# Reordering VectorE and pacing the dummy matmuls in the first slots of a fused attention and ternary FFN kernel

## The reference

```python
def xattn(x, context):                       # IMG_LEN = 257 > 128 rows: all context rows are "image" rows
    q = rms_norm(linear(x, q_w, q_b), norm_q_w).reshape(B, L, 16, 32)
    k = rms_norm(linear(context, k_img_w, k_img_b), norm_k_img_w).reshape(B, -1, 16, 32)
    v = linear(context, v_img_w, v_img_b).reshape(B, -1, 16, 32)
    return linear(softmax(q @ k.T / sqrt(32)) @ v, o_w, o_b)      # the text part has no rows

def ternary(w):                              # groups of 64 weights
    scale = clip(mean(abs(w), group), 1e-08, None)
    return clip(round(w / scale), -1, 1) * scale

x = x + tanh(g_xattn) * xattn(layernorm(x), ctx)
h = square(relu(layernorm(x) @ ternary(W_fc).T))                  # 512 -> 2048
x = x + tanh(g_ffn) * (rms_norm(h) @ ternary(W_proj).T)           # 2048 -> 512
```

## Time and profile before

| | |
|---|---|
| median of 3 runs | 1003.59 us (1002.85 to 1004.45) |
| profiled execution, its own time | 1004.31 us |
| its span from first to last instruction | 1002.5 us |
| mean granted TensorE clock | 0.973 of full speed |
| PE busy | 928.4 us (93%) |
| PEld busy | 570.9 us (57%) |
| DVE busy | 689.4 us (69%) |
| ACT busy | 717.6 us (72%) |
| POOL busy | 565.7 us (56%) |
| chain that ended last | PE 82%, issue 6%, DVE 4%, ACT 4%, POOL 2%, DMA 1% |

### The profile page before, as it was taken

One profiled execution on the slowest core, in us unless ns is written; L12 is line 12 of the kernel. 1 busy time (PEld: TensorE's weight loads), 2 busy tenths in 40 slices (PEclk: granted clock), 3 DMA queues, 4 the chain that ended last, 5 costly groups with the idle time before them and its releaser, 6 DMA issues.

```text
span 1002.5 us, 26078 instructions
## 1 busy us (share of the span) xinstructions
PE 928.4 (93%) x9941; PEld 570.9 (57%) x10043; DVE 689.4 (69%) x1360; ACT 717.6 (72%) x1235; POOL 565.7 (56%) x616
## 2 busy tenths in 40 slices
PE   3676687899999999999999999999999999999998
PEld 1343344566656566666656656666665666666664
DVE  7988987876767676777677676767777676766400
ACT  2877766677777777777777777778777777776673
POOL 1223323755666566765657565766656665766484
PEclk9887887999999999999999999999999999999999
DMA  8635333333233444343323344433342344322100
GB/s 303 168 97 147 96 86 63 64 73 77 68 72 75 86 85 75 77 80 74 80 64 73 77 85 85 75 77 84 67 79 69 72 78 86 65 54 54 43 22 32
DMA packets 184588, 82.43 MB, mean 82 GB/s; under 512 B 170000, under 2 KB 170000, under 8 KB 182928
## 3 DMA queue, kind: packets, MB, share of 16 engines
q1 hardware_dynamic: 184464, 80.77, 35.9%
HBM read 30.67 MB, written 8.39 MB: 39 GB/s over the span
## 4 chain that ended last, share of the span: by engine, by line
PE 82%; issue 6%; DVE 4%; ACT 4%; POOL 2%; DMA 1%; SPq 0%; DVEq 0%; POOLq 0%; ACTq 0%
PE mix_ps L440 11%; PE up_pair L426 10%; PE up_pair L427 10%; PE mix_ps L439 8%; PE score_ps L395 7%; PE score_ps L397 7%; PE score_ps L396 7%; PE tr_a L395 3%; PE tr_a L396 3%; PE tr_a L397 3%; PE score_ps L510 2%; PE score_ps L487 2%; PE mix_ps L577 2%; DMA big<-in_wq_t 1%; PE tr_a L440 1%
## 5 line engine op out<-in xcount | busy, mean ns | idle before, releaser
L426 PE MATMUL up_pair<-ft,w 128*128 128x256 f16 x960 | 217.1, 275 | 0.6 <-ACT h_sb L798 0.6
L427 PE MATMUL up_pair<-ft,w 128*128 128x256 f16 x960 | 217.1, 275 | 0.0
L1635 POOL TENSOR_TENSOR k_weighted<-k_raw,qk_norm 128x512 f32<-128x512 f32 x32 | 41.8, 1308 | 254.9 <-DVE k_raw L1164 253.3
L440 PE MATMUL mix_ps<-w,big 128*128 128x512 bf16 x464 | 176.1, 380 | 10.0 <-issue 8.6
L1649 POOL TENSOR_TENSOR big<-h_sb,big 128x512 f16<-128x512 f32 x128 | 155.2, 1212 | 15.6 <-ACT h_sb L807 11.2
L1659 POOL TENSOR_TENSOR hh_sum<-hh_sum,hh_sb 128x512 f32<-128x512 f32 x112 | 154.5, 1380 | 3.1 <-ACT hh_sb L820 3.1
L439 PE MATMUL mix_ps<-w,big 128*128 128x512 bf16 x382 | 145.1, 380 | 0.0
L869 ACT ACTIVATE score_ps<-score_ps,log_p,exp_scale 128x512 f32<-128x512 f32 x128 | 95.6, 747 | 58.8 <-PE score_ps L513 58.8
L1076 DVE TENSOR_TENSOR p_lo<-score_ps,p_hi 128x512 f16<-128x512 f32 x128 | 88.1, 689 | 47.6 <-ACT p_hi L751 47.0
L798 ACT ACTIVATE h_sb<-up_pair,relu_scale 128x512 f32<-128x512 f32 x120 | 81.2, 677 | 35.2 <-PE up_pair L427 34.5
L426 PEld LDWEIGHTS up_pair<-ft,w 128*128 128x128 bf16 x960 | 94.5, 98 | 18.4 <-ACT h_sb L798 1.0
(11 more groups left out here) (223 smaller groups left out, 2325.9 us busy)
## 6 DMA issues: line engine op xcount, KB each, us to landing
x_sb<-in_x SPq DMA_DIRECT2D x32, 256.0 KB, 3.0
ctx_sb<-in_ctx_t SPq DMA_DIRECT2D x32, 256.0 KB, 2.7
out<-out_sb SPq DMA_DIRECT2D x32, 256.0 KB, 2.0
big<-in_w_fc_t SPq DMA_DIRECT2D x4, 1024.0 KB, 5.2
big<-in_w_proj_t SPq DMA_DIRECT2D x4, 1024.0 KB, 5.0
big<-in_wq_t SPq DMA_DIRECT2D x1, 1024.0 KB, 7.8
big<-in_wk_t SPq DMA_DIRECT2D x1, 1024.0 KB, 9.8
big<-in_wv_t SPq DMA_DIRECT2D x1, 1024.0 KB, 10.3
```

The costliest lines, as they stand in the source:

```text
L426: nc.tensor.matmul(dst[:, half], w, ft[i][:, c, :], start=(c == 0), stop=False)
L427: last = nc.tensor.matmul(dst[:, half], w, ft[i][:, C + c, :], start=False, stop=(c == C - 1))
L440: last = nc.tensor.matmul(dst[:, :], ht_lo[i][:, row], w2[:, m, :], start=False, stop=(m == M - 1))
```

## The change

Everything changed lies between the end of slot 0 and the end of slot 4.

- TensorE: at the end of slots 0, 1 and 2, a new `warm_to_rows` waits for q's low part and issues 8 dummy matmuls. In slots 1 to 4 the 10 or 12 dummies between `scores` and `tops_t` become 9, in threes, each three waiting for one more of the first three maxima (`warm_tops`).
- ScalarE: in slots 3 and 4 `top_pairs` goes ahead of `context_hi`.
- VectorE, end of slots 1 and 2: `q_lo` and `v_lo` go to the front, right behind `attention`, and `next_rows`, `context_top` and `context_scale` follow them. The last products and the last clip of the slot go to the next slot.
- VectorE, slots 2 to 4: the last clip of the slot before now stands behind the four maxima, and the products that were put off stand where the slot has its other ternary work. In slots 3 and 4 `next_context` goes from behind `q_lo` to behind `k_out`, and `v_lo` goes ahead of `next_rows`.

```diff
+            def warm_tops(t):
+                for b in range(3):
+                    pe.wait_ge(top_ready, 4 * t + b + 1)
+                    warm(3)
+
+            def warm_to_rows(t):
+                pe.wait_ge(qlo_ready, t + 2)
+                warm(8)
...
             def early_slot(t):          # TensorE
                 scores(t)
                 ternary_pair(p)
-                warm(10)
+                warm_tops(t)
                 tops_t(t)
...
                 ternary_pair(p + 3)
+                warm_to_rows(t)
...
             def middle_slot(t):         # TensorE
                 scores(t)
                 ternary_half(n)
-                warm(12)
+                warm_tops(t)
                 tops_t(t)
...
             def middle_slot(t):         # ScalarE
                 ternary(12 if s == 2 else 15)
+                top_pairs(t)
                 context_hi(t + 1, (t + 1) % 2)
-                top_pairs(t)
...
             def early_slot(t):          # VectorE
                 score_tops(t)
+                if t > 1:
+                    ternary_clip(p - 1)
                 ternary_mask(p - 1)
                 tops_t(t)
...
                 context_lo(t + 1, (t + 1) % 2)
-                ternary_products(p - 1)
-                ternary_clip(p)
+                if t > 1:
+                    ternary_products(p - 2)
+                else:
+                    ternary_products(p - 1)
+                    ternary_clip(p)
...
                 attention(t, 1)
+                q_lo(t + 1)
+                v_lo_of(t + 1)
+                next_rows(t + 2)
+                context_top(t + 2)
+                context_scale(t + 2, (t + 2) % 3)
+                if t > 1:
+                    ternary_mask(p)
+                    ternary_products(p)
                 ternary_clip(p + 1)
...
-                ternary_products(p + 2)
-                ternary_clip(p + 3)
...
             def middle_slot(t):         # VectorE
                 score_tops(t)
+                if s == 2:
+                    ternary_clip(p - 1)
+                else:
+                    ternary_half(n - 1)
                 ternary_mask(p - 1)
                 tops_t(t)
                 context_lo(t + 1, (t + 1) % 2)
+                if s == 2:
+                    ternary_products(p - 2)
                 ternary_products(p - 1)
                 ternary_half(n)
...
                 k_out(t + 1)
+                next_context(t + 2)
                 x1_stats(s, s)
...
                 x_lo(t + 2)
                 ternary_products(p + 1)
-                if s == 2:
-                    ternary_half(n + 5)
```

More of the change, by code:

```diff
@@ L593, in first_slot @@
                 ternary_pair(2)
+                warm_to_rows(0)
             def early_slot(t):
@@ L1390, in early_slot @@
                 context_lo(t + 1, (t + 1) % 2)
-                ternary_products(p - 1)
-                ternary_clip(p)
+                if t > 1:
[3 more added lines that the diff above has]
+                    ternary_clip(p)
                 probs_lo(t, 0)
-                ternary_mask(p)
+                if t > 1:
+                    ternary_signed(p - 1)
+                else:
+                    ternary_mask(p)
                 probs_lo(t, 1)
-                ternary_signed(p)
+                if t > 1:
+                    ternary_final(p - 1)
+                else:
+                    ternary_signed(p)
                 x1_out(s, s)
@@ L1399, in early_slot @@
                 probs_lo(t, 3)
-                ternary_final(p)
+                if t > 1:
+                    ternary_clip(p)
+                else:
+                    ternary_final(p)
                 k_out(t + 1)
@@ L1409, in early_slot @@
                 attention(t, 1)
+                q_lo(t + 1)
[3 more added lines that the diff above has]
+                context_scale(t + 2, (t + 2) % 3)
+                if t > 1:
+                    ternary_mask(p)
+                    ternary_products(p)
                 ternary_clip(p + 1)
-                q_lo(t + 1)
                 ternary_mask(p + 1)
                 normed_lo(s)
-                next_rows(t + 2)
                 attention_lo(t)
                 ternary_products(p + 1)
-                v_lo_of(t + 1)
-                context_top(t + 2)
-                context_scale(t + 2, (t + 2) % 3)
+                x_lo(t + 2)
                 ternary_clip(p + 2)
                 ternary_mask(p + 2)
-                x_lo(t + 2)
-                ternary_products(p + 2)
-                ternary_clip(p + 3)
             def middle_slot(t):
@@ L1451, in middle_slot @@
                 normed_lo(s)
+                q_lo(t + 1)
                 ternary_half(n + 3)
-                q_lo(t + 1)
-                next_context(t + 2)
+                v_lo_of(t + 1)
                 next_rows(t + 2)
```

## The result

The changed kernel takes 1008.69 us (median of 5 runs, 1006.44 to 1009.80); the kernel before took 1002.85 us in the 5 runs beside it (1002.10 to 1004.45). The ratio is 1.0054, interval 1.0038 to 1.0070: slower, where 1001.4 us was forecast and 1004.2 was the upper end of the range. The profiled execution took 1008.56 us, its span is 1006.7 us, and its mean granted clock is 0.973 as before.

The account below looks back on a forecast made before the run. Slots 1 to 4 were taken as bound by a path from VectorE to the maxima, then TensorE, ScalarE, VectorE, TensorE. Terms summed to 2.65 us off 1004.3 us, 1001.7; adjusted for a faster execution, forecast 1001.4 us, range 998.6 to 1004.2.

Parts of the forecast that it names:

- End of slot 1: End of slot 1 to slot 2's transpose: VectorE reaches the maxima 1.5 us sooner; lead 2.4 us, between 1.4 and 2.8.
- lead: Followed through slots 0 to 5: how far the new times are ahead of the old; 2.7 us at slot 5's maxima.
- End of slot 2: VectorE, end of slot 2: exchanged products, clip and wait bring it to slot 3's maxima 0.5 us later; lead 1.9 us.
- the wait for v's high part (0.2 us): VectorE, ends of slots 1 and 2: v_lo directly behind q_lo waits for v's high part, losing about 0.2 us.
- The late group sums: TensorE, starts of slots 3 and 4: group sum waits for a clip now behind the maxima; costs 2.0 and 1.95 us.
- Rest of slot 3: After slot 3's transpose: context maximum moved, wait for x's high rows goes; gain 3.1 us, less 0.7 us for piece 9.
- Rest of slot 4: After slot 4's transpose: context maximum leaves, 1.90 us wait for x's high rows goes; gain 2.5 us.
- They hide nothing, and the lead stays to the end: Slot 5 onward: TensorE's FFN products end when the maxima did, so the 2.7 us lead passes to the end.
- The sum: Slots 1 to 4: all terms added give 2.65 us gained against the profiled 1004.3 us, so 1001.7 us; forecast 1001.4 us.
- 12 in 100 rival: TensorE between scores and transpose, slots 3 and 4: costs up to 6.2 us; slower, about 1005.5 us; chance 12 in 100.
- signs for being right: Profile after: late dummies in slots 3 and 4, waits gone, clock 1.00, slot 2's maxima 1.5 us sooner, slot 5's over 2.
- The sign for being wrong: Profile after: slot 3 no shorter than 34.6 us; also changed slots from 7 on, or VectorE waits over 1.5 us.

Follow-up runs that it names:

- e12: Changed kernel with v's low part of slots 1 and 2 moved behind context_scale; 1002.72 us, -0.09% against before.
- e1: Changed kernel with the clips back ahead of the maxima in slots 3 and 4; 1002.69 us, -0.08% against before.
- e13: e8 with v's low part of slots 1 and 2 moved behind context_scale; 993.34 us, -0.95% against before.
- e9: Changed kernel without the nine dummies of slots 3 and 4; 1004.37 us, +0.02% against before.
- e3: Changed kernel with GpSimd's additions of squared hidden rows in slots 3 and 4 cut to 2 of 512 columns; 1002.48 us, -0.07% against before.
- e4: Kernel before with only the context maximum of slots 3 and 4 moved behind k_out; 1001.16 us, -0.19% against before.
- e5: e1 with q's and v's low parts of slots 3 and 4 back in the old order; 1001.79 us, -0.20% against before.
- e7: e4 with the slot 5 dummies of e2; 999.44 us, -0.43% against before.
- e10: e7 with threes paced by the maxima in place of the twelve dummies of slots 3 and 4; 998.45 us, -0.49% against before.
- e11: e10 with TensorE's eight dummies ending slots 0 to 2 and paced threes in slots 1 and 2, VectorE in old order; 996.87 us, -0.71% against before.
- e2: Changed kernel with 8 dummies and three paced threes in slot 5's wait; 1004.24 us, +0.16% against before.
- e6: Changed kernel with slots 3 and 4 as before and slot 2 ending as before; 1004.03 us, +0.06% against before.
- e8: e5 with the slot 5 dummies of e2; 1000.20 us, -0.40% against before.

## Why the prediction was wrong, by its steps

**End of slot 1: right in the number, and in part by luck.** 2.1 to 2.4 us of lead were forecast at slot 2's transpose; apart from the 1.0 us from slot 0 it was 2.3. But 1.2 us of it came at the start of slot 1, where 0.3 were forecast and the clock was back at 67.7 us for 68.9 before, and VectorE's wait for v's high part was 1.17 us here too, where 0.2 stood in the sum; e12 shows what it cost, 1.6 us in rest 1.

**End of slot 2: mis-sized.** The term was +0.5 us, and +1.2 came in the profile, with 4.6 us at half clock behind the transpose on both sides; e1 against e13 puts the price of the wait, and what hangs on it, at 1.8. The step that failed is "the wait for v's high part (0.2 us)". It was set against the 1.75 us that `q_lo` took in the earlier trace rows. That 1.75 was a stretched operation; in its new place `q_lo` takes 0.83 us, and the 0.9 us it gave back turned into a wait of 1.17 us for the same event.

**The late group sums: right in size, and too mild in rank.** 2.0 and 1.95 us were forecast, 2.0 and 2.0 measured. With e1 and e9 the whole loss against before is gone, though neither is faster than before: the ratio moves by 0.62 and 0.52 percentage points (6.2 and 5.2 us). Against the changed kernel the tops are 5.3 and 5.6 us shorter and the rests of slots 3 and 4 take 1.6 and 1.4 back. Slot 5 is 1.3 and 1.1 us shorter (29.46 and 29.66 us for 30.78), but not by a shorter wait. TensorE at slot 5's transpose in e1:

```profile
196.52 0.48 PE L498 MATMUL tr_a<-ident,m_rows 128*128 128x128 f32 x1 [4.76 <-ACT m_rows L870]
```

The wait is 4.76 us there and 4.68 in e9, as in the changed kernel; the stretch at half clock was 3.4 us in these two and 6.8 in the changed kernel. e9 corrects the name of the fault: not the late sum but the block of dummies behind it. e3 takes 6.1 us off as well with the late sums left as they are, so this place is not the only one that decides.

**Rest of slot 3: mis-sized by 0.6 us.** -2.4 forecast with the products of piece 9, -1.8 measured. The context maximum is worth 2.1 of it (e4), as the prediction's argument had it. The collision described next is here too: the second product took 1.53 us for 0.69, and e3 gives 1.0 back.

**Rest of slot 4: the step that failed.** It said that the wait of 1.90 us goes and that the gain is 2.5 us. The wait went (0.58 left), the context maximum gives 1.0 us alone (e4), and yet the stretch grew by 0.4. The prediction looked only at what VectorE waited for and not at what it would then run beside. Measured in its place: 1.9 us more in two products beside GpSimd (e3 gives back 1.4), and v's low part ahead of x's rows (e5 gives back 1.1). The collision comes with the move of the context maximum alone: e4, e7, e10 and e11 have the pair at 1.75 and 1.53 us too, and their rests 4 are 28.4 to 28.5 us. So what sets the changed kernel apart from them in this stretch, 1.3 to 1.4 us, is the rest of its new order there, of which e5 sizes v's and q's low parts.

**"They hide nothing, and the lead stays to the end": the other step that failed, 2.7 us.** A lead of TensorE and not of VectorE is idle time in slot 5. It was 4.68 us, the clock fell, and the 5.8 us behind it ran at half speed; e1, e9 and e12 had the same wait and lost 1.4, 1.6 and 2.3 us, so the wait has no fixed price. e2 takes it away: 28.05 us. The prediction had tied an idle TensorE to the clock in slots 1 to 4 and did not ask the same of slot 5, where the earlier trace rows begins its "nothing to spare" only later.

**The sum.** From 2.65 us ahead to 5.2 us behind at slot 6 are 7.9 us: 1.0 in slot 0, 0.7 in the end of slot 2, 0.6 in the rest of slot 3, 2.9 in the rest of slot 4, 2.7 in slot 5. That is the 12 in 100 rival, "slower" at about 1005.5 us: its place and its condition (rests of slots 3 and 4 under 3 us together; they gave 1.82 - 0.37 = 1.45) are what happened, its price lacked slot 5.

**The signs.** Of the signs for being right, five came: the first dummy behind the fourth maximum, the transpose 6.0 and 6.5 us after the maxima begin, no wait for the context maximum, 0.58 us of wait for x's high rows at the end of slot 4 and none at the end of slot 3, and a clock of 1.00 ahead of the third `ffn_up`. Slot 2's maxima began 1.17 us sooner and not 1.5, and slot 5's 2.5 us later and not 2 sooner. The sign for being wrong, slot 3 no shorter than 34.6 us, came (`scores` at 119.14 and 159.19 us, 40.0 us), but is a poor one: v's low part brought slot 3's `scores` forward by 3.7 us and not its maxima.

**What stays open.** The trace's 1.0 us in slot 0 has no experiment; e4, e7 and e10, with the old code there, have slot 1's maxima at 63.74, 65.30 and 65.20 us, so it may be nothing but the difference of two executions. e12's executions fall into two groups, eight of 1001.5 to 1004.0 us and three of 1005.0 to 1005.8. The profiled one is of the second and has 30.31 us in slot 5; whether the others have less there was not seen. Stretches of one execution move by 1 to 2 us between kernels with the same code in them (rest 2), so terms under that size are sizes of one execution, and only the ratios of the whole are firm.

## What to carry to other kernels

Filler instructions paced by an engine are worth something only if nothing ahead of them in their queue waits for that same engine; else they are released together and stand in the path, 2 us a slot here. When a wait is taken away, ask what the freed engine runs beside and who now idles: a gain of 1.3 us in a wait went into products beside GpSimd, and TensorE's lead into a slot at half clock. An operation moved ahead to be early must not itself wait for something later than the work it passes.

## What the runs showed of the hardware

- A VectorE product of 128x1024 bf16 took 0.68 us in a gap of GpSimd's and 1.53 to 1.76 us beside GpSimd operations without gaps between them; it took 0.68 us again when the addition beside it was cut to 2 columns (e3).
- Behind a wait of 4.68 us TensorE did 5.8 us of work at a granted clock of 0.50, and with 17 dummy matmuls put into the wait slot 5 was 2.7 us shorter and the whole 3.8 us. The same wait in the same place was followed by half clock of another length in other kernels: 3.4 us in all in e1 and e9, 6.8 in the changed kernel and e12. Behind waits of 2.69 us (e3) and 1.50 us (e6) there the clock stayed at 1.00.
- The eight dummies at the end of slot 1 took 1.46 us in e13 and 2.65 us in e8. The wait just before was 1.99 and 2.00 us: the clock stayed up in the one and fell at 86.2 us in the other.
